# Weight loads between token tiles, gate weights behind the first projections, small loads moved to the last sequence

## The chip, the cores and the metric

The kernel runs on one core of a Trainium2 chip. The metric is device time in microseconds (us): the median of several executions. Engines are named as in the profile: PE (TensorE matmul), PEld (its weight load), DVE (VectorE), ACT (ScalarE), POOL (GpSimd), SP (SyncE, which here only issues transfers), and the 16 DMA engines.

## The reference, cut to what matters

```
x = x + window_attention(layernorm(x))            # 8 sequences of 512 tokens, width 256, 16 heads
x = x + cross_attention(layernorm(x), ctx, mask)
x = x + ffn(layernorm(x))

def ffn(x):                                       # attention runs over the 8 sequences at each position
    y = layer_norm(x + mha(x, Wqkv, bqkv, Wo, bo), g1, be1)
    logits = y @ Wg.T                             # 8 experts
    idx = argmax(logits)
    moe = relu(y @ W1[idx] + b1[idx]) @ W2[idx] + b2[idx]
    return layer_norm(y + moe, g2, be2)
```

All arithmetic is in float32, or in float32 split into bfloat16 parts. The kernel gets the gate's logits without y: it multiplies the gate weights into the output projection beforehand (`w_o[:, :, D:GATED]`, the "gated" columns) and sums them up (`gate_sums`).

## The kernel before, in words

Three programs follow one another, each a block in which the five engines run their own instruction lists and meet only at semaphores.

**Attention** (`attention_program`) goes over the sequences n = 0 to 7. SP issues all transfers in the order of its `iteration(n)`: the copy of the prefix values, the context, x for the layernorm two sequences ahead, x for the residual (`x_res`), the rows of the cross attention's queries (`stack_context_queries`), the rows of queries and keys of the first half of the heads of the next sequence (`stack_front(n, 0)`), the mask, one fill of the table `sorted` with empty rows (`fill_rows`, 4290 KB a time), the shift rows of the next sequence (`stack_shift`, two small transfers that PE's `window_shifted(n + 1, 0, 0)` waits for), the second half of the heads, and the context's keys. In sequence 0 the 31 loads of the next stage's constants (`later_loads`) stand between the mask and the fill, L529 to L531. ACT issues two small transfers of its own in each sequence (L1111, shift rows of the second half of the heads, for `window_shifted(n, 2, 0)`). Sequence 0 has no cross attention; that of sequence 7 and the tail of the window attention run in `closing`.

**Mixing** (`mixing_program`) goes over 8 groups of 512 tokens, n = 0 to 7, in a software pipeline. In `iteration(n)` PE does the transposes (`features`), the output projection of the group before (`output(n)`), queries and keys, `heads`, values, the scores of group n + 1 and the ranks that sort tokens by expert. DVE does the softmax, adds the residual (`mix`), takes layernorm statistics and chooses the expert; POOL takes rstd and logits and sends finished rows by indirect DMA (`send_rows`, four instructions for a group, on table positions that DVE's `slots` computes). PE, ACT and DVE pass results through two PSUM banks in a fixed order of names, `work_order`: a fill may start when the fill two places before it is read (`work_claim`).

Before group 0 stands the opening: `gate_weights()` on PE (transposes of w_o, L2489; totals, L2494; gated product, L2499), for which ACT takes the transposed w_o out of PSUM (`take_gates`, L2422) after it has written the position mask (L2444), which POOL makes; then 14 matmuls whose result nobody reads (`keep_warm(14)`, L2508), `features(-1)`, four projections and values of group 0. SP loads x of group m by eight transfers (`load_x`, L2017), each after DVE has normalised the group before, and the weights of expert n (`load_expert`, 2 MB in three transfers) after x of group n + 3. All experts must have landed before DVE builds the step tables that end the stage.

The last two groups run without a successor: PE goes through `output(7)`, `heads(7)`, `ranks(7)`, `output(8)`, and then the ranks in two halves; DVE's `last_route` does the same two halves.

**Experts** (`expert_program`) runs 39 steps of 128 rows each, PE-bound.

Of the kernel before, what the change touches and what calls it, by code (L numbers as in the profile page):

```python
# [142 lines left out]
def attention_program(nc, t, mem, later_loads, x_in, group_loaded, x2_stored, waits_passed):  # L143
# [3 lines left out]
    with ctx:  # L147
# [256 lines left out]
        with nc.Block() as block:  # L404

            @block.sync
            def _(sp):
# [88 lines left out]
                def tiles_of(src):  # L496
                    return src.rearrange("(c p) d -> p c d", p=P)
# [5 lines left out]
                def fill_rows(dst, count):  # L503
                    sp.dma_start(dst, filler[:, :].unsqueeze(1).broadcast_to([P, count, ROW])).then_inc(rows_filled.sem, 16)

                def iteration(n, last=False, ahead=True):
                    first = isinstance(n, int) and n == 0
                    copy_prefix(n)
                    if not first:
                        sp.wait_ge(ctxT_ready.sem, ctxT_ready.count(n, 0))  # L510
                    for rep in range(2):
                        sp.dma_start(ctx_in[rep * CTX:(rep + 1) * CTX, :], t["ctx"][n]).then_inc(ctx_loaded.sem, 16)
                    if ahead:
                        sp.wait_ge(ln_done.sem, ln_done.next(n, TILES))
                        load_x(n + 2)
                    if not first:
                        sp.wait_ge(x1_ready.sem, x1_ready.count(n, 2))
                    sp.dma_start(x_res[:, :, :], tiles_of(t["x"][n])).then_inc(xres_loaded.sem, 16)
                    if not first:
                        for tile in range(KD):  # L520
                            stack_context_queries(n, tile)
                    if not last:
                        stack_front(n, 0)
                    if not first:
                        stack_shift2(n)
                    if not first:
                        sp.wait_ge(mask_ready.sem, mask_ready.count(n, 1))
                    sp.dma_start(mask_in[:, :, :], tiles_of(t["mask"][n])).then_inc(mask_loaded.sem, 16)
                    if first:  # L529
                        for dst, src in later_loads:  # L530
                            sp.dma_start(dst, src).then_inc(later_loaded.sem, 16)  # L531
                        sp.wait_ge(consts_set.sem, 12)
                    fill_rows(t["sorted"][0:E * REGION, :].rearrange("(e p k) w -> e p k w", e=E, p=P)[n], REGION // P)
                    if last:
                        fill_rows(t["sorted"][E * REGION:, :].rearrange("(p k) w -> p k w", p=P), SPARE_TILES)
                    if not last:
                        stack_shift(n)
                        stack_front(n, 1)
                    if not first and not last:
                        store_x2(n)  # L540
                    split_context_keys(n)
# [1197 lines left out]

N_CONST = 6 + 5 + 4  # L1740
REGION = B * S + P
SPARE_TILES = 10
# [16 lines left out]
ROUTE_FILLS = ["out0", "out1", "out2", "out3", "ranks"]  # L1759
HALVES_FILLS = ["out0", "out1", "out2", "out3", "ranks0", "ranks1"]  # L1760
GATED = D + E
PROJECT_FILLS = ["xT0", "xT1", "q0", "q1", "k0", "k1", "v0", "v1", "v2", "v3"]
MIX_FILLS = ["xT0", "xT1", "out0", "out1", "out2", "out3", "q0", "q1", "k0", "k1", "v0", "v1", "v2", "v3", "ranks"]
OPENING_FILLS = [f for f in MIX_FILLS if f not in ROUTE_FILLS]
CLOSING_FILLS = [f for f in MIX_FILLS if f not in PROJECT_FILLS]
QUADS, QUAD = 4, 32
# [67 lines left out]
def mixing_program(nc, t, mem, consts, keep, ahead, x_in, group_loaded, x2_stored, waits_passed):  # L1834

    ctx = ExitStack()
    with ctx:
# [126 lines left out]
        def released(n, name):  # L1964

            kind, k = name.rstrip("0123"), int(name[-1]) if name[-1] in "0123" else 0
            sig, count = {
                "xT": (xT_ready, KD + k + 1), "q": (q_ready, KD + k + 1), "k": (k_ready, KD + k + 1),
                "v": (v_ready, TILES + k + 1), "out": (mixed_ready, k + 1), "ranks": (next_row_ready, k + 1),
            }[kind]  # L1970
            return sig.sem, sig.count(n, count)
# [6 lines left out]
        def work_filled(n, name):  # L1978

            return sum(len(work_order(m)) for m in range(-1, n)) + work_order(n).index(name) + 1  # L1980

# [4 lines left out]
        def work_claim(pe, n, name):  # L1986

            order = work_order(n)
# [21 lines left out]
        with nc.Block() as block:  # L2010

            @block.sync
            def _(sp):
# [13 lines left out]

                def iteration(n, more):
                    if more:
                        sp.wait_ge(ln_done.sem, ln_done.count(n, 3 * TILES))  # L2030
                        load_x(n + 3)
                    load_expert(n)

                sp.dma_start(keep["b1"][:, :], t["e_b1"]).then_inc(weights_loaded.sem, 16)
                sp.dma_start(tile_rows[:, :], t["c_tile_rows"]).then_inc(weights_loaded.sem, 16)
                sp.wait_ge(x2_stored.sem, x2_stored.count(B, 16))
                for m in range(2):
                    sp.wait_ge(ln_done.sem, ln_done.count(m, TILES))
                    load_x(m + 1)
                for n in range(NGROUPS):  # L2040
                    iteration(n, n < NGROUPS - 3)

# [112 lines left out]
            def _(dve):  # L2155
# [134 lines left out]
                def iteration(n, more=True):  # L2290
                    route = n > 0
                    shift_scores(n)
                    if n > 1:
                        slots(n - 1, whole, 0, "ranks")
# [3 lines left out]
                    if route:  # L2298
                        mix(n, 1)
                        mix(n, 2)  # L2300
                    normalise(n)
                    if route:
                        mix(n, 3)
                    turn(n)
                    keep_gate(n)
# [11 lines left out]
                def last_route(n):  # L2317
                    first_half, second_half = post_norm_parts(n)
                    for k, own in enumerate((first_half, second_half)):
                        for c in range(own.start, own.stop):  # L2320
                            mix(n, c)
                        post_norm_statistics(n, own)
                        post_norm_scale(n, own)
# [49 lines left out]
                for n in range(NGROUPS):  # L2373
                    iteration(n, more=n < NGROUPS - 2)
                slots(NGROUPS - 1, whole, 0, "ranks")
                last_route(NGROUPS)
# [3 lines left out]
            def _(act):  # L2380
# [37 lines left out]

                def take_gates():
# [4 lines left out]
                    act.wait_ge(gates_summed.sem, 2)  # L2424
                    nc.scalar.activation(w_o[:, :, D:GATED], ps_heads[:, 1, 0:KD * E].rearrange("p (k e) -> p k e", k=KD),
                                         ACT.Copy).then_inc(gates_ready.sem, 1)
                    nc.scalar.activation(gate_sums[:, :, :], ps_heads[:, 2, 0:3 * E].rearrange("p (i e) -> p i e", i=3),
                                         ACT.Copy).then_inc(gates_ready.sem, 1)

                def iteration(n, project=True):  # L2430
# [7 lines left out]
                    if project:  # L2438
                        values(n)

                act.wait_ge(mask_made.sem, 3)
                for r in range(QUADS):
                    own = slice(QUAD * r, QUAD * (r + 1))
                    nc.scalar.activation(mask_pos[own, :], own_position[own, :, :].rearrange("p i s -> p (i s)")[:, own],  # L2444
                                         ACT.Copy).then_inc(mask_made.sem, 1)
                take_gates()
                act.wait_ge(consts_set.sem, CONSTS_SET)
                features(-1)
                queries(-1)
                keys(-1)  # L2450
                values(-1)
                for n in range(NGROUPS):
# [6 lines left out]
            def _(pe):  # L2459
# [24 lines left out]

                def gate_weights():
# [5 lines left out]
                    mm.then_inc(gates_summed.sem, 1)  # L2491
                    pe.wait_ge(gates_made.sem, 4 * KD + 1)
                    for k in range(KD):
                        nc.tensor.matmul(ps_heads[:, 2, 0:3 * E], ones, gates[:, k, :, :].rearrange("p i e -> p (i e)"),  # L2494
                                         start=(k == 0), stop=(k == KD - 1), skip_group_check=True)
                    pe.wait_ge(gates_ready.sem, 1)
# [52 lines left out]

                def output(n):  # L2550
                    for c in range(TILES):
                        ps = work_claim(pe, n, f"out{c}")
# [23 lines left out]
                def iteration(n, project=True, route=True):  # L2576
# [12 lines left out]
                    if route:  # L2589
# [392 lines left out]
```

## Time and profile before

| what | value |
|---|---|
| median of 3 runs (lowest, highest) | 1214.45 us (1211.98, 1217.58) |
| profiled execution: own time, its span | 1213.34 us, 1211.3 us |
| busy: PE, DVE, ACT, POOL | 1112.3 (92%), 734.5, 478.9, 510.3 us |
| first instruction of mixing, of experts | 691.88 us, 912.45 us |
| fill of `sorted`, 4290 KB: median from issue to landing | 17.3 us |
| one row transfer `q_rows<-q_parts`, 128 KB | 2.4 us |
| one tile transfer `x_in<-x_rows`, 64 KB | 2.4 us |

Times inside the span count from its first instruction. In a row of the timeline the first number is the start, the second the duration, then engine, line, operation, what is written and read, and the number of instructions (x3); brackets give the idle time of that engine just before, and what ended it. A letter q behind an engine (SPq, ACTq) is its queue that issues transfers: the duration there is that of issuing.

### The profile page before, as it was taken

What the parts mean: (1) busy time and instruction counts of PE and PEld (TensorE: products, weight loads), DVE (VectorE), ACT (ScalarE), POOL (GpSimd) and SP (SyncE); (2) the same over time, 40 slices, a digit from 0 to 9 for tenths busy, and PEclk for the clock granted to TensorE, in tenths of its full rate; (3) what the DMA queues carried; (4) which work ended last, traced back from release to release, by engine and by line L of the source; (5) the groups of instructions that cost most, each with busy time, mean ns of one, the idle gap of its engine ahead of it and who ended that gap; (6) DMA issues with size and microseconds to landing.
All of it is one profiled execution on the core that took longest, in us unless ns stands there. A gap on an engine that the chain in (4) does not pass through costs nothing. (4 is left out here: it accounts for less than half of the span.)

```text
span 1211.3 us, 29502 instructions
## 1 busy us (share of the span) xinstructions
PE 1112.3 (92%) x10067; PEld 753.3 (62%) x10068; DVE 734.5 (61%) x2088; ACT 478.9 (40%) x866; POOL 510.3 (42%) x758
## 2 busy tenths in 40 slices
PE   8998899999999999999988889998879999999995
PEld 3545455464464554645554446656548999999994
DVE  4554676657756667576536436666574556566563
ACT  5444545454544545444452233233203333333330
POOL 3324425235244252442522022445363665556654
PEclk9999999999999999999999989889989999999998
DMA  7256563735546546336363113537213111111110
GB/s 220 71 155 166 147 188 106 201 102 144 154 116 173 155 112 189 102 106 189 105 182 88 56 36 98 183 107 273 78 51 93 50 49 50 49 51 56 50 44 7
DMA packets 143477, 137.95 MB, mean 114 GB/s; under 512 B 30376, under 2 KB 136750, under 8 KB 143280
## 3 DMA queue, kind: packets, MB, share of 16 engines
q1 hardware_dynamic: 137808, 124.20, 36.0%
q0 software_dynamic: 5280, 12.66, 3.2%
q8 instruction: 43, 0.70, 0.2%
q14 instruction: 26, 0.21, 0.1%
q10 hardware_dynamic: 320, 0.16, 0.1%
HBM read 49.38 MB, written 50.83 MB: 83 GB/s over the span
## 5 line engine op out<-in xcount | busy, mean ns | idle before, releaser
L970 ACT ACTIVATE probs<-ps_ab 128x512 f32<-128x512 f32 (+2 forms) x352 | 174.5, 537 | 95.3 <-PE ps_ab L1292 39.4
L591 POOL TENSOR_SCALAR_AFFINE_SELECT probs<-probs 128x512 f32<-128x512 f32 x128 | 81.7, 638 | 271.1 <-ACT probs L970 267.4
L2854 PE MATMUL ps_ab<-e_yT,e_w_now 128*128 128x128 f32 x1248 | 146.6, 276 | 0.0
L2854 PEld LDWEIGHTS ps_ab<-e_yT,e_w_now 128*128 128x128 f32 x1248 | 143.3, 193 | 0.5 <-ACT e_yT L2825 0.4
L2865 PE MATMUL ps_c<-keep_w,e_hT 128*128 x624 | 141.0, 379 | 0.0
L2865 PEld LDWEIGHTS ps_c<-keep_w,e_hT 128*128 128x128 f32 x624 | 115.7, 190 | 14.1
L712 DVE CUSTOM_DVE_ANT_0 ps_ab<-ps_ab,mask_qk 128x256 f32<-128x256 f32 x224 | 89.0, 451 | 18.8 <-PE ps_ab L1261 18.7
L1822 ACT ACTIVATE e_w_now<-keep_w 128x1024 f32 x78 | 78.2, 1049 | 40.1 <-issue 40.1
L706 DVE TENSOR_REDUCE top<-ps_ab 128x2 f32<-128x512 f32 (+1 forms) x112 | 74.2, 684 | 28.8 <-PE ps_ab L1261 28.0
L2789 DVE TENSOR_SCALAR e_hT<-ps_ab,keep_b 128x128 f32<-128x128 f32 x312 | 84.4, 343 | 8.5 <-PE ps_ab L2854 6.0
L1261 PE MATMUL ps_ab<-k_rows,q_rows 96*128 96x256 bf16 (+1 forms) x512 | 84.5, 260 | 4.6 <-DVE top L712 2.7
L2825 ACT ACTIVATE e_yT<-ps_d 128x256 f32<-128x256 f32 x39 | 15.0, 384 | 168.3 <-PE ps_d L2844 168.3
L1292 PE MATMUL ps_ab<-q_rows,k_rows 98*128 98x256 bf16 (+1 forms) x512 | 75.5, 260 | 0.2
L578 POOL TENSOR_TENSOR parts<-rest,parts 128x512 bf16<-128x512 f32 x32 | 38.0, 1189 | 82.7 <-ACT parts L960 82.7
L1261 PEld LDWEIGHTS ps_ab<-k_rows,q_rows 96*128 96x128 bf16 x512 | 39.9, 98 | 45.5 <-DVE top L712 12.3
L2766 POOL DMA_INDIRECT out<-e_result,e_token x39 | 41.8, 1072 | 60.5 <-DVE e_token L2785 43.9
L1335 PE MATMUL ps_c<-probs,v_ones 128*32 128x256 f32 (+1 forms) x1024 | 64.4, 359 | 0.0
L1219 PE MATMUL ps_d<-xT,w_qkv 128*128 128x512 f32 x128 | 62.6, 607 | 0.2
L2473 PE MATMUL ps_d<-e_w_now,m_w_qkv 128*128 128x512 f32 x128 | 56.4, 594 | 1.5 <-ACT e_w_now L2398 1.5
L594 POOL TENSOR_SCALAR_AFFINE_SELECT probs<-probs 128x256 f32<-128x256 f32 x128 | 56.7, 443 | 0.0
L2801 DVE TENSOR_TENSOR e_summed<-ps_c,e_yb 128x256 f32<-128x256 f32 x39 | 16.6, 425 | 62.9 <-PE ps_c L2865 62.9
L766 DVE RECIPROCAL rden<-rden 128x512 f32<-128x512 f32 x15 | 50.1, 3342 | 7.0 <-ACT rden L1000 7.0
(250 smaller groups left out, 2137.6 us busy)
## 6 DMA issues: line engine op xcount, KB each, us to landing
sorted_rows<-filler SPq DMA_DIRECT2D x8, 4290.0 KB, 17.3
q_rows<-parts SPq DMA_DIRECT2D x96, 128.0 KB, 2.4
k_rows<-parts SPq DMA_DIRECT2D x96, 128.0 KB, 2.4
q_rows<-q_parts SPq DMA_DIRECT2D x96, 128.0 KB, 2.4
keep_w<-in_e_w SPq DMA_DIRECT2D x16, 512.0 KB
keep_w<-in_e_w SPq DMA_DIRECT2D x8, 1024.0 KB
e_row<-sorted_rows SPq DMA_DIRECT2D x39, 130.0 KB, 2.1
x_in<-in_x SPq DMA_DIRECT2D x8, 512.0 KB, 3.9
```

The lines of the kernel that those rows point to most:

```text
L591: nc.gpsimd.affine_select(own, own, [[0, TILES], [1, P]], ALU.is_ge, keep_zero, base=0, channel_multiplier=-1).then_inc(probs_cut.sem, 1)
L706: nc.vector.tensor_reduce(top[:, c, first:first + heads], ps.rearrange("p (h k) -> p h k", h=heads), AX.X, ALU.max).then_inc(max_free.sem, 1)
L712: best = nc.vector.tensor_tensor_reduce(scores, scores, mask_qk[:, 1, :], 1.0, LEAST, ALU.add, ALU.max, top[:, c, first + i:first + i + 1])
L970: nc.scalar.activation(probs[:, user % 2, lo:lo + width], ps_exp[:, f % 2, 0:width], ACT.Exp).then_inc(exp_done.sem, 1)
L1219: mm = nc.tensor.matmul(ps, w_qkv[:, k, col:col + P], xT[:, k, :], start=(k == 0), stop=(k == KD - 1), skip_group_check=True)
L1261: mm = nc.tensor.matmul(ps[:, i * width:(i + 1) * width], q_rows[0:SPLIT_ROWS, k, q0:q0 + P], k_rows[0:SPLIT_ROWS, k, q0 + P - width:q0 + ...
L1292: mm = nc.tensor.matmul(ps[:, 256 * i:256 * i + q1 - q0], k_rows[:, h, kt * P:(kt + 1) * P], q_rows[:, h, q0:q1], start=(kt == 2), stop=Tr ...
L1335: mm = nc.tensor.matmul(ps_out[32 * j:32 * j + 32, g % 2, q0:q1], lhsT, rhs, start=(kt == order[0]), stop=True, skip_group_check=True)
L1822: nc.scalar.activation(self.w1_now[:, s, k, :], keep["w1"][:, k, bass.ds(e * DF, DF)], ACT.Copy).then_inc(self.w1_ready.sem, 1)
L2789: nc.vector.tensor_scalar(hT[:, s, f, :], ps_h[s][:, f // 4, (f % 4) * P:(f % 4 + 1) * P], b1[:, bass.ds(e * KF + f, 1)], 0.0, ALU.add, AL ...
L2854: mm = nc.tensor.matmul(ps_h[s][:, f // 4, (f % 4) * P:(f % 4 + 1) * P], w1_now[:, s, k, f * P:(f + 1) * P], yT[:, s, k * P:(k + 1) * P], ...
L2865: mm = nc.tensor.matmul(ps_out[:, s, 0:D], hT[:, s, f, :], w2[:, bass.ds(e * KF * D + f * D, D)], start=(f == 0), stop=(f == KF - 1))
```

## The change

Four parts: (1) the constants' loads leave sequence 0 and go in two lots, 13 and 18, around the queries' rows of sequence 7; (2) the gate weights are made in two steps, the product behind the first four projections, and ACT takes w_o before the mask; (3) SP loads the weights of expert n + 1 when `features(n)` are taken, and x of group n + 3 behind them; (4) in the last group DVE turns the probabilities before it mixes the third tile, and PE does half of `output(8)` before `ranks(7)`, with the fills and DVE's `slots(7)` moved to match.

```diff
@@ attention, SP, iteration(n)
                     sp.dma_start(x_res[:, :, :], tiles_of(t["x"][n])).then_inc(xres_loaded.sem, 16)
+                    if last:
+                        load_later(later_loads[:EARLIER])          # EARLIER = 13
                     if not first:
                         for tile in range(KD):
                             stack_context_queries(n, tile)
+                    if last:
+                        load_later(later_loads[EARLIER:])
...
                     if first:
-                        for dst, src in later_loads:
-                            sp.dma_start(dst, src).then_inc(later_loaded.sem, 16)
                         sp.wait_ge(consts_set.sem, 12)
@@ mixing, order of the PSUM fills
-HALVES_FILLS = ["out0", "out1", "out2", "out3", "ranks0", "ranks1"]
+HALVES_FILLS = ["out0", "out1", "ranks_held", "out2", "out3", "ranks0", "ranks1"]
-CLOSING_FILLS = [f for f in MIX_FILLS if f not in PROJECT_FILLS]
+CLOSING_FILLS = ["out0", "out1", "out2", "out3"]
@@ mixing, SP
-                for m in range(2):
-                    sp.wait_ge(ln_done.sem, ln_done.count(m, TILES))
-                    load_x(m + 1)
-                for n in range(NGROUPS):
-                    iteration(n, n < NGROUPS - 3)     # load_x(n + 3) after ln_apply(n + 2), then load_expert(n)
+                sp.wait_ge(ln_done.sem, ln_done.count(0, TILES))
+                load_x(1)
+                for n in range(-1, NGROUPS - 1):
+                    sp.wait_ge(xT_ready.sem, xT_ready.next(n, KD))
+                    load_expert(n + 1)
+                    if n < NGROUPS - 3:
+                        sp.wait_ge(ln_done.sem, ln_done.count(n, 3 * TILES))
+                        load_x(n + 3)
@@ mixing, DVE, iteration(n), closing = n == NGROUPS - 1
                     if route:
                         mix(n, 1)
+                        if not closing:
+                            mix(n, 2)
+                    normalise(n)
+                    if closing:
+                        turn(n)
                         mix(n, 2)
-                    normalise(n)
                     if route:
                         mix(n, 3)
-                    turn(n)
+                    if not closing:
+                        turn(n)
@@ mixing, DVE, last_route
                             mix(n, c)
+                        if k == 0:
+                            slots(n - 1, whole, 0, "ranks")
@@ mixing, ACT, opening
+                take_w_o_back()            # w_o transposed, and the totals
+                act.wait_ge(consts_set.sem, CONSTS_SET)
+                features(-1)
                 act.wait_ge(mask_made.sem, 3)
                 for r in range(QUADS):
                     ...                    # position mask
-                take_gates()
-                act.wait_ge(consts_set.sem, CONSTS_SET)
-                features(-1)
                 queries(-1)
                 keys(-1)
+                take_gated_w_o()
                 values(-1)
@@ mixing, PE, opening
-                gate_weights()
+                turn_w_o()
+                gate_totals()
                 keep_warm(14)
                 features(-1)
                 for j in range(4):
                     query_or_key(-1, j)
-                pe.wait_ge(gates_made.sem, 4 * KD + 1)
+                gated_w_o()
                 projected_values(-1)
@@ mixing, PE, end
-                output(NGROUPS)
+                output(NGROUPS, (0, 1))
+                ranks(NGROUPS - 1)         # before: at the end of iteration(NGROUPS - 1)
+                output(NGROUPS, (2, 3))
```

## Rows read from the trace of the kernel before

**Rows 1.** Timeline of SP's queue, sequence 0, behind the mask.
```profile
67.01 0.55 SPq L531 DMA_DIRECT2D m_identf<-in_c_identity  x1
...
84.77 0.65 SPq L504 DMA_DIRECT2D sorted_rows<-filler  x1
88.78 7.31 SPq L473 DMA_DIRECT2D q_rows<-shiftT  x2
```

**Rows 2.** Timeline of SP's queue, the same two steps in sequence 1.
```profile
149.71 0.66 SPq L504 DMA_DIRECT2D sorted_rows<-filler  x1
166.50 1.42 SPq L473 DMA_DIRECT2D q_rows<-shiftT  x2
```

**Rows 3.** Timeline of PE: start and a later step of sequence 1, then of sequence 2.
```profile
102.37 0.23 PE L1288 MATMUL ps_ab<-mask_first,ident 128*128 128x128 bf16 x1 [4.05 <-DMA q_rows<-shiftT]
...
129.38 0.28 PE L1299 MATMUL ps_ab<-mask_prefix,ident 128*128 128x256 bf16 x1 [0.21 <-ACT probs L970]
...
182.82 0.22 PE L1288 MATMUL ps_ab<-mask_first,ident 128*128 128x128 bf16 x1
...
209.04 0.28 PE L1299 MATMUL ps_ab<-mask_prefix,ident 128*128 128x256 bf16 x1 [0.20 <-ACT probs L970]
```

**Rows 4.** Busy times by window: length, PE, PEld, DVE, ACT, POOL, granted clock, DMA share, GB/s.
```profile
102.40:107.50 5.10, 5.02 (x30) 3.89 (x31) 0.68 (x2) 3.35 (x7) 2.00 (x4) 0.67 0.92 211
```

**Rows 5.** Timeline of ACT's queue and of PE, sequence 0, second half of the heads.
```profile
66.58 1.93 ACTq L1111 DMA_DIRECT2D q_rows<-shiftT  x2
...
72.28 0.22 PE L1288 MATMUL ps_ab<-mask_first,ident 128*128 128x128 bf16 x1
```

**Rows 6.** Timeline of SP's queue in sequence 7, and of PE at its queries' second tile.
```profile
590.71 0.59 SPq L518 DMA_DIRECT2D x_res<-in_x  x1
598.14 7.74 SPq L461 DMA_DIRECT2D q_rows<-q_parts  x12
616.16 1.22 SPq L467 DMA_DIRECT2D q_rows<-shiftT  x2
...
610.74 0.38 PE L1419 MATMUL ps_ab<-mask_add,ident 128*128 128x512 bf16 x1 [0.28 <-DVE top L738]
```

**Rows 7.** Timeline of PE, DVE and ACT in the opening of mixing.
```profile
693.34 0.62 PE L2494 MATMUL ps_ab<-m_gates,e_w_now 128*128 128x24 f32 x4 [0.50 <-DVE m_gates L2218]
...
696.57 1.62 DVE L109 TENSOR_SCALAR m_xn<-x_in,m_moments,m_rstd 128x256 f32<-128x256 f32 x4 [1.44 <-POOL m_rstd L103]
...
698.77 0.60 ACT L2422 ACTIVATE e_w_now<-ps_ab 128x512 f32<-128x512 f32 x1
...
699.42 1.88 PE L2499 MATMUL ps_ab<-m_gates,e_w_now 128*128 128x8 f32 x8 [5.45 <-ACT e_w_now L2422]
...
701.15 4.79 PE L2508 MATMUL ps_c<-m_before,m_ident 128*128 128x512 bf16 x14
...
707.61 4.56 PE L2473 MATMUL ps_d<-e_w_now,m_w_qkv 128*128 128x512 f32 x10 [0.80 <-ACT e_w_now L2398]
```

**Rows 8.** Busy times by window, columns as in rows 4: the opening, then two groups.
```profile
699.40:705.60 6.20, 6.18 (x22) 3.41 (x23) 0.00 (x0) 0.27 (x2) 1.43 (x2) 0.59 0.30 89
...
826.10:850.00 23.90, 20.68 (x330) 14.25 (x327) 15.87 (x51) 7.18 (x13) 10.76 (x16) 0.93 0.98 344
850.00:872.70 22.70, 20.63 (x326) 14.12 (x324) 12.58 (x39) 7.18 (x13) 9.79 (x14) 0.92 0.20 69
```

**Rows 9.** Timeline of DVE's statistics of groups 1 and 2, and PE's group 1.
```profile
705.60 1.40 DVE L92 BATCH_NORM_STATS2 m_stats<-x_in 128x6 f32<-128x256 f32 x4 [7.41 <-DMA x_in<-x_rows]
...
724.60 1.40 DVE L92 BATCH_NORM_STATS2 m_stats<-x_in 128x6 f32<-128x256 f32 x4
...
735.47 1.09 PE L2466 MATMUL ps_d<-m_identf,m_xn 128*128 128x128 f32 x8
```

**Rows 10.** Timeline of DVE in the last two groups.
```profile
876.43 0.43 DVE L2208 TENSOR_TENSOR m_mixed<-ps_d,m_xnb 128x264 f32<-128x264 f32 x1 [0.32 <-PE ps_d L2556]
...
893.79 0.88 DVE L2250 SCALAR_TENSOR_TENSOR m_rows<-m_mixed,m_rstd,m_be 128x256 f32<-128x256 f32 x2 [2.07 <-POOL m_rstd L2083]
```

More of the change, by code:

```diff
@@ L504, in fill_rows, with load_later @@
                     sp.dma_start(dst, filler[:, :].unsqueeze(1).broadcast_to([P, count, ROW])).then_inc(rows_filled.sem, 16)
+                def load_later(loads):
+                    for dst, src in loads:
+                        sp.dma_start(dst, src).then_inc(later_loaded.sem, 16)
                 def iteration(n, last=False, ahead=True):
@@ L1740 @@
 N_CONST = 6 + 5 + 4
+EARLIER = 13
 REGION = B * S + P
@@ L1969, in released @@
                 "v": (v_ready, TILES + k + 1), "out": (mixed_ready, k + 1), "ranks": (next_row_ready, k + 1),
+                "ranks_held": (next_row_ready, 0),
             }[kind]
@@ L1978, in work_filled @@
         def work_filled(n, name):
+            if name == "ranks" and n == NGROUPS - 1:
+                n, name = NGROUPS, "ranks_held"
             return sum(len(work_order(m)) for m in range(-1, n)) + work_order(n).index(name) + 1
@@ L1986, in work_claim @@
         def work_claim(pe, n, name):
+            if name == "ranks" and n == NGROUPS - 1:
+                n, name = NGROUPS, "ranks_held"
             order = work_order(n)
@@ L2026, in load_expert @@
                                  t["e_w2"][e].rearrange("(j p) d -> p j d", p=P)).then_inc(weights_loaded.sem, 16)
[L2028 to L2032, printed above, removed]
                 sp.dma_start(keep["b1"][:, :], t["e_b1"]).then_inc(weights_loaded.sem, 16)
@@ L2292, in iteration @@
                     shift_scores(n)
+                    closing = n == NGROUPS - 1
                     if n > 1:
@@ L2374, in _ @@
                     iteration(n, more=n < NGROUPS - 2)
-                slots(NGROUPS - 1, whole, 0, "ranks")
                 last_route(NGROUPS)
@@ L2417, in values, with take_w_o_back @@
                         nc.scalar.activation(v[:, c, :], ps[:, 0:GATED], ACT.Copy).then_inc(v_ready.sem, 1)
-                def take_gates():
+                def take_w_o_back():
                     act.wait_ge(gates_summed.sem, 1)
@@ L2424, in take_gates, with take_gated_w_o @@
                     act.wait_ge(gates_summed.sem, 2)
+                    nc.scalar.activation(gate_sums[:, :, :], ps_heads[:, 2, 0:3 * E].rearrange("p (i e) -> p i e", i=3),
+                                         ACT.Copy).then_inc(gates_ready.sem, 1)
+                def take_gated_w_o():
+                    act.wait_ge(gates_summed.sem, 3)
                     nc.scalar.activation(w_o[:, :, D:GATED], ps_heads[:, 1, 0:KD * E].rearrange("p (k e) -> p k e", k=KD),
-                                         ACT.Copy).then_inc(gates_ready.sem, 1)
-                    nc.scalar.activation(gate_sums[:, :, :], ps_heads[:, 2, 0:3 * E].rearrange("p (i e) -> p i e", i=3),
                                          ACT.Copy).then_inc(gates_ready.sem, 1)
@@ L2483, in projected_values, with turn_w_o @@
                         mm.then_inc(work_full.sem, 1)
-                def gate_weights():
+                def turn_w_o():
                     for j in range(KD):
@@ L2491, in gate_weights, with gate_totals, gated_w_o @@
                     mm.then_inc(gates_summed.sem, 1)
+                def gate_totals():
                     pe.wait_ge(gates_made.sem, 4 * KD + 1)
                     for k in range(KD):
-                        nc.tensor.matmul(ps_heads[:, 2, 0:3 * E], ones, gates[:, k, :, :].rearrange("p i e -> p (i e)"),
-                                         start=(k == 0), stop=(k == KD - 1), skip_group_check=True)
+                        mm = nc.tensor.matmul(ps_heads[:, 2, 0:3 * E], ones, gates[:, k, :, :].rearrange("p i e -> p (i e)"),
+                                              start=(k == 0), stop=(k == KD - 1), skip_group_check=True)
+                    mm.then_inc(gates_summed.sem, 1)
+                def gated_w_o():
                     pe.wait_ge(gates_ready.sem, 1)
@@ L2548, in heads, with output @@
                     mm.then_inc(heads_full.sem, 1)
-                def output(n):
-                    for c in range(TILES):
+                def output(n, tiles=range(TILES)):
+                    for c in tiles:
                         ps = work_claim(pe, n, f"out{c}")
@@ L2588, in iteration @@
                         scores(n + 1)
-                    if route:
+                    if route and project:
                         ranks(n)
```

## The prediction

> **What bounds the kernel now.** I read the page first: PE is busy for 92% of the span, so the question at each edit is whether PE stands still there, and for what. The chain that ended last lies wholly in the expert stage, which the change does not touch; any gain must come before it and shift it. The waits of PE and the timelines by stage then show two standstills that the change aims at. In sequence 1 PE starts with 4.05 us of waiting for the shift rows [rows 3]; in the opening of mixing it waits 5.45 us for ACT's copy of w_o [rows 7]. Both are followed by a low clock: 0.67 in the 5.1 us behind the first [rows 4], 0.59 in the 6.2 us behind the second [rows 8]; 2.4 GHz is granted elsewhere, 1.2 GHz in parts of these.
>
> **Part 1, the constants' loads.** In sequence 0 the 31 loads take SP from 67.01 to 84.77, 17.76 us, 0.57 each. Only then is the fill issued; 4.0 us later SP starts the shift rows, which take 7.31 us to issue behind it [rows 1]. In sequence 1 the fill goes out 16.8 us before the shift rows, and their issue takes 1.42 us [rows 2]. Without the loads the fill of sequence 0 is issued at about 67.0 and, at its 17.3 us, has landed at 84.3, before 88.78. Issued in 1.4 us and landing 2.4 us later (the figure of the other row transfers), the shift rows are there at 92.6; PE wants them at 98.3 (102.37 less 4.05). So the wait goes as a whole: 4.05 us. The clock: from its first instruction to L1299 sequence 1 takes 27.01 us, sequence 2 takes 26.22 [rows 3]; the 0.79 us between them is the low clock as far as PE's other partners let it count. Bounds for the two together: 4.05 (no clock gain), and 4.05 + 5.1 x 0.33 = 5.7 (all of it). I take 4.8, from the comparison of like sequences.
>
> In sequence 7 the first 13 loads (7.4 us) start at 591.30 and end at 598.7 to 599.2, so the queries' rows start 0.6 to 1.1 us late. Their last is now issued by 605.88 and used from 610.74 [rows 6]: 4.9 us less 2.4 of landing leaves 2.5, enough. The 18 others (10.3 us) end near 617.2, so the shift rows of 616.16 start about 1 us late; what is late next are the mask, the two last fills and the context's keys, all issued behind them for PE work of the closing. I cost this at nothing; if the cover were gone it costs its 1.1 us.
>
> **Part 2, the gate weights.** ACT now takes w_o first, so PE goes on from the totals, which end at 693.96, straight into the 14 matmuls. These took 4.79 us at a clock of 0.59; I keep that, and they end at 698.75. The normalised x is ready at 696.57 + 1.62 = 698.19, so it no longer matters. From the end of the 14 to the first projection it was 707.61 - 705.94 = 1.67 us; the first projection moves to 700.42, by 7.2 us [rows 7]. The product stands now behind the projections and costs PE time there: eight instructions, 1.88 us at the low clock, 1.24 if they run like the totals (four in 0.62) [rows 7]. I take 1.24, since the clock is full from 705.6 on. ACT's copies of the mask (four) fall between x and the first query, while PE runs 1.7 us of projection. Net 5.9 us. Bounds: at full clock the 14 end before 698.19 and x decides, 0.56 more, 6.5; if the low clock reaches into the projections for some 3.5 us, that costs 1.7 and the product its 1.88: 3.5 to 3.8, lower bound 3.5.
>
> **Part 3, the weights.** In the steady groups nothing moves: after x of a group SP finds `features` taken and issues one expert as before, only two experts further on. What changes is both ends. At the start expert 0 goes out behind x of group 1 (from about 704), ahead of x of group 2, which is requested when group 1 is normalised, near 710.4. In the group where four experts were issued together the DMA engines moved 344 GB/s [rows 8]; at that rate 2 MB take 6.1 us and are through by 713, so x of group 2 meets only the end of it. x of group 1 came 7.4 us after its request (698.19 to 705.60 [rows 9]), so x of group 2 lands at 717.8, with the weights at 720 at worst. DVE wants it at 724.60 - 5.9 = 718.7; its statistics and scaling need 4.8 us, and PE wants the result at 735.47 - 5.9 = 729.6 [rows 9]. Slack 4.8 us: nothing is lost. At the end the four experts are no longer issued at once. The group beside that burst lasts 23.9 us, the next 22.7, with the same 20.6 to 20.7 us of PE work [rows 8]. Bounds 0 and 1.2 us; I take 0.6, for its granted clock was no lower.
>
> **Part 4, the last groups.** DVE no longer waits 0.32 us for the third output before it normalises [rows 10]; turning one `mix` (0.43) earlier brings PE's `heads(7)` and half of `output(8)` forward by some us. But in the last group DVE stands 2.07 us for POOL's rstd before 893.79 [rows 10]. POOL is busy until then with the six sends that its list puts ahead of that rstd, and this part takes none of them away; only their start, behind DVE's statistics, moves by the 0.32. Also `slots(7)`, now behind two `mix` (0.9 us), is done 2 us or more before that rstd. I take 0.3 us; bounds 0 and 0.8.
>
> **Sum.** 4.8 + 5.9 + 0.6 + 0.3 = 11.6 us off the execution that was profiled, 1213.34 us (span 1211.3 and 2.0 around it): 1201.7. The median of the runs shown is 1.1 higher, so the forecast is 1202.8 us. With all lower bounds the sum is 7.5 (1207), with all upper ones 14.2 (1200.3). A measurement here tells a change from none at about 0.5%, 6.1 us.
>
> **Rivals.**
> (a) *The clock keeps half of it.* The low clock moves onto the projections, and the stretch behind the first wait gains nothing: 4.05 + 3.5 + 0 to 0.6, so 1206 to 1207. For it: both standstills were followed by low clock although PE was busy in it. Against: the new opening has no PE gap of more than half a microsecond behind 693.96. Chance 0.12.
> (b) *x comes late.* The fill moves 4290 KB in 17.3 us, 248 GB/s. If weights from memory got half of that beside the tiles, 2 MB would take 17 us, x of group 2 (512 KB) would land near 727, its result at 732, 2.4 us after PE wants it, and group 3's may repeat it: 2.4 to 6 us, 1205 to 1209. Against it: x of group 1 is issued ahead of all weights. Chance 0.07.
> (c) *The other side: the early fill stops ACT's shift rows.* ACT issues them from 66.58 to 68.51 and PE uses them at 72.28 [rows 5]; the new fill is issued at 67.0. Behind a fill on SP's own queue the like pair took 7.31 us to issue and held PE up [rows 1, 3]. If ACT's pair had to wait it out as well, it would land after 84.3 and PE stand 12 us, and lose 1.7 of clock: 1216.5. It decides from a stall of 11.6 us up; one of 2 to 3 us costs just that. Against it: it is another queue, and half of the pair is issued before the fill. Chance 0.05.
> The Trainium skill, "DMA: Bandwidth & Descriptors", section "Queues, rings and completion order", says that a DMA engine takes turns between its queues, one whole packet of descriptors each (9 to 17 typical, 64 at most). By that rule the pair waits for a packet or two of the fill, not for all of it; no row here has the two side by side, and the sum would stay.
> (d) *The groups give it back.* In both groups of rows 8 PE idles for 2 to 3 us and the clock falls (23.90 less 20.68, 22.70 less 20.63) [rows 8]. If the new phase lengthens that by 1 to 2 us in each of five groups, 5 to 9 us return: 1207 to 1211. Nothing in the change moves the sends against the scores within a group. Chance 0.07.
>
> **How the numbers follow.** Forecast, 1199 to 1207: 0.66; (a) 0.12, (b) 0.07, (c) 0.05, (d) 0.07, and 0.03 for a slowdown over 0.5% that I do not see. The range 1197.5 to 1208.5 takes in (a), most of (b) and half of (d), and leaves out about 0.15. Faster by over 0.5% (below 1208.4): 0.66 + 0.12 + 0.05, and 0.01 of (d): 0.84. Within: 0.12. Slower: 0.04.
>
> **What would show it.** Right: no DMA wait of PE at the start of sequence 1, SP's two shift transfers issued in under 2 us, PE's first L1288 there at 98.3 and not 102.37; PE without a gap over 1 us between the totals and the first projection, that one at about 695.6 (4.8 + 7.2 earlier); x of group 2 awaited by DVE for no more than 2 us; experts starting near 901. Wrong: a PE wait for shift rows near 72, a gap before `features(1)` in mixing, more PE idle time in the later groups, or a DMA wait of PE in sequence 7.

## The result, and the profile after

| | before | changed |
|---|---|---|
| median of 10 runs (lowest, highest) | 1216.67 us (1211.98, 1218.13) | 1207.41 us (1203.19, 1208.41 and one of 2705) |
| profiled execution: own time, its span | 1213.34, 1211.3 us | 1207.58, 1205.6 us |
| first `features(1)` matmul of mixing | 735.47 us | 726.43 us |
| ranks of group 6 (`ranks(6)`) | 872.49 us | 866.57 us |

The ratio is 0.9926, 95% interval 0.9912 to 0.994: 9.0 us off (7.3 to 10.7), where 11.6 were forecast. The ratio leaves out the one execution of the changed kernel that took 2705 us; the median of its nine others is 1207.25. The two profiled executions stand only 5.7 us apart, since that of before was low among its runs. Two lines of the page of the changed kernel:

```profile
span 1205.6 us, 29501 instructions
...
PE 1113.7 (92%) x10067; PEld 754.1 (63%) x10068; DVE 734.2 (61%) x2088; ACT 478.6 (40%) x866; POOL 509.7 (42%) x758
```

PE is as busy as before; what moved is where it stands still. The timelines of SP, ACT and PE in sequences 0 and 1 of the changed kernel, against [rows 1, 3, 5]:

```profile
67.21 0.63 SPq L504 DMA_DIRECT2D sorted_rows<-filler  x1
91.64 1.49 SPq L473 DMA_DIRECT2D q_rows<-shiftT  x2
...
66.54 1.93 ACTq L1117 DMA_DIRECT2D q_rows<-shiftT  x2
...
74.17 0.29 PE L1294 MATMUL ps_ab<-mask_first,ident 128*128 128x128 bf16 x1 [1.78 <-DMA q_rows<-shiftT]
...
101.02 0.22 PE L1294 MATMUL ps_ab<-mask_first,ident 128*128 128x128 bf16 x1
...
127.20 0.28 PE L1305 MATMUL ps_ab<-mask_prefix,ident 128*128 128x256 bf16 x1 [0.21 <-ACT probs L976]
...
144.12 0.39 PE L1262 MATMUL ps_ab<-mask_qk,ident 128*128 128x512 bf16 x1 [1.65 <-DMA k_rows<-parts]
...
612.97 0.23 PE L1294 MATMUL ps_ab<-mask_first,ident 128*128 128x128 bf16 x1 [0.70 <-DMA q_rows<-shiftT]
```

The fill goes out at 67.2, SP's shift rows take 1.49 us to issue, and the wait of 4.05 us at the start of sequence 1 is gone. But a new one stands at 74.17: ACT's pair is behind the fill. The packets of its second transfer run from 70.4 to 73.1 us, where in the kernel before they were through by 69.4. So PE is at L1305 only 2.2 us sooner (127.20 for 129.38). The row at 144.12 is a wait that every kernel has (before: 1.45 us at 146.10); the last one, in sequence 7, is new.

The opening of mixing, timeline of PE and one row of DVE, against [rows 7, 9]:

```profile
691.15 0.62 PE L2518 MATMUL ps_ab<-m_gates,e_w_now 128*128 128x24 f32 x4 [0.50 <-DVE m_gates L2227]
691.62 3.18 PE L2536 MATMUL ps_c<-m_before,m_ident 128*128 128x512 bf16 x14
694.85 1.97 PE L2487 MATMUL ps_d<-m_identf,m_xn 128*128 128x128 f32 x8
697.61 7.13 PE L2494 MATMUL ps_d<-e_w_now,m_w_qkv 128*128 128x512 f32 x16 [0.80 <-ACT e_w_now L2414]
704.58 0.95 PE L2527 MATMUL ps_ab<-m_gates,e_w_now 128*128 128x8 f32 x8
...
726.43 1.09 PE L2487 MATMUL ps_d<-m_identf,m_xn 128*128 128x128 f32 x8
...
702.77 1.41 DVE L92 BATCH_NORM_STATS2 m_stats<-x_in 128x6 f32<-128x256 f32 x4 [6.77 <-DMA x_in<-x_rows]
```

From the totals to `features(1)` it is 35.28 us, before 42.13: 6.85 off. The 14 unread matmuls run in 3.18 us, not 4.79: with no standstill ahead of them the clock stays at 2.4 GHz (1.00 from 691.6 to 694.9).

With 9.04 us in hand at 726.43 the changed kernel has 5.92 left at `ranks(6)`. The windows view of one of the groups between, and its scores in the timelines of PE and POOL:

```profile
795.40:820.20 24.80, 22.28 (x327) 15.31 (x324) 15.77 (x51) 7.18 (x13) 10.91 (x16) 0.84 0.39 126
```
```profile
815.35 0.69 PE L2555 MATMUL ps_c<-e_w_now 64*32 64x32 f32 x43
816.50 0.28 PE L2555 MATMUL ps_c<-e_w_now 64*32 64x32 f32 x6 [0.45 <-issue]
817.24 0.25 PE L2555 MATMUL ps_c<-e_w_now 64*32 64x32 f32 x4 [0.47 <-issue]
818.15 0.33 PE L2555 MATMUL ps_c<-e_w_now 64*32 64x32 f32 x3 [0.66 <-issue]
818.87 1.12 PE L2555 MATMUL ps_c<-e_w_now 64*32 64x32 f32 x72 [0.40 <-issue]
...
813.03 1.12 POOL L2125 DMA_INDIRECT sorted_rows<-m_rows,m_slot  x1 [0.64 <-issue]
814.45 0.96 POOL L2125 DMA_INDIRECT sorted_rows<-m_rows,m_slot  x1 [0.30 <-issue]
815.72 0.96 POOL L2125 DMA_INDIRECT sorted_rows<-m_rows,m_slot  x1 [0.30 <-issue]
816.99 0.96 POOL L2125 DMA_INDIRECT sorted_rows<-m_rows,m_slot  x1 [0.30 <-issue]
```

"issue" means that the profile names nothing that PE waited for. The 128 small matmuls of `scores` stop four times, while POOL sends rows; then the clock falls and the next group's first matmuls run at half speed. Before had this too: up to `ranks(6)` such gaps in the scores add up to 9.5 us in 17 pieces there, and to 10.3 us in 19 after, 1.2 of it in `scores(2)`. The five groups from `ranks(1)` to `ranks(6)` take 118.2 us before, 119.8 after, and the group ahead of them 19.0 and 20.6. So in the five groups the gaps are no longer than before (9.1 us for 9.5); PE idles for 13.3 us in them for 13.4, and is busy 1.7 us longer (106.5 for 104.8), at a granted clock of 0.90 for 0.91.

In the last group DVE waits 4.92 us for POOL's rstd, where it had waited 2.07 [rows 10]; the statistics came earlier, POOL's answer did not:

```profile
887.60 0.88 DVE L2259 SCALAR_TENSOR_TENSOR m_rows<-m_mixed,m_rstd,m_be 128x256 f32<-128x256 f32 x2 [4.92 <-POOL m_rstd L2092]
```

### The profile page after: what moved, and what is told of

Same layout as the page of the kernel before. It is cut to its first block and busy times, and to the rows that moved or that the text cites. A ratio compares the mean times of both kernels' runs of the same rounds, so it can differ in the third digit from the quotient of the medians.

```text
span 1205.6 us, 29501 instructions
## 1 busy us (share of the span) xinstructions
PE 1113.7 (92%) x10067; PEld 754.1 (63%) x10068; DVE 734.2 (61%) x2088; ACT 478.6 (40%) x866; POOL 509.7 (42%) x758
## 5 line engine op out<-in xcount | busy, mean ns | idle before, releaser
L2896 PEld LDWEIGHTS ps_c<-keep_w,e_hT 128*128 128x128 f32 x624 | 115.7, 190 | 14.1
L1298 PEld LDWEIGHTS ps_ab<-q_rows,k_rows 98*128 98x128 bf16 x512 | 41.9, 99 | 21.3 <-ACT probs L976 9.4
```

Source lines behind the costliest of these rows:

```text
L1298: mm = nc.tensor.matmul(ps[:, 256 * i:256 * i + q1 - q0], k_rows[:, h, kt * P:(kt + 1) * P], q_rows[:, h, q0:q1], start=(kt == 2), stop=Tr ...
L2896: mm = nc.tensor.matmul(ps_out[:, s, 0:D], hT[:, s, f, :], w2[:, bass.ds(e * KF * D + f * D, D)], start=(f == 0), stop=(f == KF - 1))
```

## The experiments

Times off are ratios times the median of before on the same chip: 1203.8 us for the first four, 1203.4 for the next four, 1215.8 for the last four; in brackets the 95% interval.

### Each part alone

The kernel before with the lines of one part of the diff.

> The kernel before with part 1 alone (the constants' loads leave sequence 0 and go in two lots in sequence 7). The prediction's step says 4.8 us less than before, and no wait of PE for shift rows near 72 us. The theory read from the trace of the changed kernel says: SP's wait of 4.05 us is gone, but ACT's second shift transfer now lands behind the fill's first packets, PE waits 1.5 to 2 us at about 74 us and runs at half clock for some 3 us behind it, and only 2.0 to 2.5 us are gained in all. A rival: the low clock after that wait is not part 1's doing but luck of the execution; then the PE wait is there and 3.0 to 3.5 us are gained.

Off: 3.5 us [1.0 to 6.0]. Timeline of PE in this kernel:

```profile
74.33 0.23 PE L1294 MATMUL ps_ab<-mask_first,ident 128*128 128x128 bf16 x1 [1.85 <-DMA q_rows<-shiftT]
...
607.88 0.39 PE L1425 MATMUL ps_ab<-mask_add,ident 128*128 128x512 bf16 x1 [0.95 <-DMA q_rows<-q_parts]
```

The new wait is part 1's. Here no low clock followed it, and L1305 comes at 126.39, 2.99 us sooner: the rival that priced it without the clock. In the interval lie that and 4.8 too; for this one execution the trace decides. The second row is a wait that I had costed at nothing: sequence 7's queries' rows, behind the 13 loads.

> The kernel before with part 2 alone (totals first, gated product behind the first projections, ACT takes w_o ahead of the mask). The prediction's step says 5.9 us less than before (3.5 to 6.5). The theory read from the trace of the changed kernel says 6.5 to 7: the 14 unread matmuls run at full clock in 3.2 us and not in 4.8. The rival by which the clock keeps half says 3.5. First projection of mixing 7 to 10 us after the totals, where before it was 14.

Off: 7.1 us [4.9 to 9.4]. The 14 matmuls take 3.18 us again, and from the totals to `features(1)` it is 35.18 us. The forecast was 1.0 low; rival (a) is out for this execution.

> The kernel before with part 3 alone (weights of an expert ahead of x of the next group but one, and no burst of four at the end). The prediction's step says 0.6 us less (0 to 1.2). The theory read from the trace of the changed kernel: the group beside the former burst is no shorter, so 0 gained there; and if the 1.5 us that group 1 lost in the changed kernel (PE idle for no named cause in the scores of group 2) come from the weights that now start there, this kernel is 1 to 1.5 us slower than before. If that loss is not part 3's, no change, within 0.3 us.

Off: 1.1 us [-1.0 to 3.3], too wide to size it. `scores(2)` runs without a gap, so the 1.2 us lost there in the changed kernel is not part 3's: that reading of mine falls. The group beside the former burst takes 20.06 us from ranks to ranks; in parts 1 and 2 alone, with the burst, 21.01 each. All these groups have the sends beside them as well, so the difference of 1 us need not be the burst's alone.

> The kernel before with part 4 alone (turn ahead of the mix of the third tile in the last group; half of the output projection of the last group ahead of its predecessor's ranks). The prediction's step says 0.3 us less (0 to 0.8). Rival from the trace of the changed kernel: PE now stands 3.2 us before the first half of the last ranks and runs its next stretch at half clock, which takes back what was gained: no change, or up to 0.5 us slower.

Off: 0.5 us [-2.0 to 2.9]. From `ranks(7)` to `ranks0` it takes 14.05 us; the five other kernels with the old order (before, parts 1, 2 and 3 alone, and the tenth run) have 14.31 to 14.41. The rival of a longer wait is half right: PE waits 3.07 us before `ranks0`, where it had waited 1.80; but from there to the second half it takes 2.19 us in both. The profiled execution, 1214.9 us, is the longest of the twelve, and its five groups from `ranks(1)` to `ranks(6)` take 116.7 us, where the first three runs have 106.3 to 109.1.

### The fill held, the sends moved

> The changed kernel itself, beside the next three on the same chip. If its parts add up (part 1 alone 3.1 us, part 2 alone 6.5 to 7.1, parts 3 and 4 together 0 to 1.6, by ratios and traces), it is 10 to 11.5 us under the kernel before; if the parts disturb each other in the groups of mixing, about 9, as in the first comparison.

Off: 9.4 us [6.1 to 12.6], with single executions from 1189.8 to 1199.1. PE's wait at 74 is 2.14 us and 6.8 us of 1.2 GHz follow it.

```diff
                     if first:
                         sp.wait_ge(consts_set.sem, 12)
+                        sp.wait_ge(shift_stacked[1].sem, shift_stacked[1].count(n, 32))
                     fill_rows(...)
```

> The changed kernel with one wait more: in sequence 0 SP issues the fill only when ACT's two shift transfers have landed, near 69.5 us. If the fill's packets are what delays the second of them, the wait of PE at 74 us (1.8 us) is gone, the next transposed rows come 1.8 to 2.9 us sooner, and the time is 1.9 us under that of the changed kernel, up to 2.9 with the clock. If the delay is ACT's queue's own, the wait stays and the time is that of the changed kernel. The fill still lands by 87 us, and SP's shift rows are issued behind it without a new wait at the start of sequence 1.

Off: 15.3 us [13.0 to 17.6], executions from 1187.5 to 1190.3. Windows view of the same 4.6 us, first the changed kernel, then this one (the last three columns are clock, DMA share, GB/s), and this one's timelines:

```profile
68.40:73.00 4.60, 3.62 (x24) 1.55 (x21) 3.65 (x7) 1.23 (x2) 1.15 (x1) 1.00 1.06 321
```
```profile
68.40:73.00 4.60, 4.22 (x31) 2.25 (x29) 3.66 (x7) 1.48 (x3) 1.15 (x1) 1.00 0.43 144
```
```profile
69.82 0.64 SPq L504 DMA_DIRECT2D sorted_rows<-filler  x1
88.72 1.92 SPq L473 DMA_DIRECT2D q_rows<-shiftT  x2
...
98.09 0.22 PE L1295 MATMUL ps_ab<-mask_first,ident 128*128 128x128 bf16 x1
...
693.05 8.83 PE L2495 MATMUL ps_d<-e_w_now,m_w_qkv 128*128 128x512 f32 x16 [0.80 <-ACT e_w_now L2415]
```

Where the fill filled the DMA engines (share 1.06, 321 GB/s) ACT's pair, 8 KB each, now finds them half idle. PE does not wait at 74 nor at 98.09, the time that the prediction gives for it (98.3). In the four kernels with the hold, L1305/6 comes at 124.28 to 124.46; in the five with the early fill (the first, fifth, seventh, eighth run and the changed kernel) at 126.39 to 128.59, mean 127.6: the early fill costs 3.2 us. At the totals, the first matmuls of mixing that use the gate weights, the same nine profiles stand at 686.6 to 688.2 and at 690.0 to 693.1: 3.9 us on average. The median here is 7.1 us under that of the changed kernel on the same chip, more than that; between the two profiles 3.6 us arise behind `ranks0`, where the two kernels are alike, and why is open. The last row shows rival (a): the 16 projections take 8.83 us and not 7.13, half clock over 3.4 us of them. It is so in this and the eleventh run; the seven other profiles of kernels with part 2 have 7.13.

```diff
                     iteration(n, ahead=n < NGROUPS - 1, more=n < NGROUPS - 2)
+                    if n < NGROUPS - 1:
+                        wait_apart(pool, pool_passed, scores_full.sem, scores_full.count(n + 1, 1))
                     send_rows(n - 1)
```

> The changed kernel, but in groups 2 to 6 POOL sends the rows of the group before only when PE has finished the scores of the next group. If PE's idle time in the scores (1 to 2.3 us a group, with no releaser named) comes from these sends, it goes, the half clock behind it too, and five groups of up to 24 us become 21 us each: 5 to 12 us under the changed kernel. If the idle time is PE's own supply of instructions, it stays, and the time is that of the changed kernel or up to 2 us more, since the sends may now hold up POOL's bias and rstd.

Off: 13.7 us [10.5 to 17.0]; its median is 7.8 us under that of the changed kernel. Windows view of a group, and its scores and sends in the timelines:

```profile
786.10:806.70 20.60, 18.88 (x328) 12.49 (x324) 16.88 (x51) 7.18 (x13) 10.95 (x16) 1.00 0.48 155
```
```profile
794.45 5.39 PE L2496 MATMUL ps_d<-e_w_now,m_w_qkv 128*128 128x512 f32 x12 [0.63 <-DVE m_mixed L2219]
...
805.16 1.42 PE L2557 MATMUL ps_c<-e_w_now 64*32 64x32 f32 x128
...
791.14 0.96 POOL L2125 DMA_INDIRECT sorted_rows<-m_rows,m_slot  x1 [0.30 <-issue]
792.12 1.28 POOL L2085 TENSOR_TENSOR m_xnb<-m_xn,m_b_o 128x512 f32<-128x512 f32 x1
```

The 128 matmuls run in one piece, the clock is 1.00 over the group, and it takes 20.6 us for 24.8 in the first profile of the changed kernel. On this chip the difference is smaller: the five groups take 101.6 us, in the fifth run 107.1. What is left of the sends is the end of the last one at 792.1, straight behind which POOL does the bias that DVE needs; PE waits 0.6 to 0.9 us for that.

```diff
-                        nc.gpsimd.indirect_dma_start(out=t["sorted"], ..., in_=rows[...]).then_inc(rows_sent[...].sem, 16)
+                        nc.gpsimd.memset(unsent[...], 0.0).then_inc(rows_sent[...].sem, 16)
```

> The changed kernel without the transfers of finished rows: POOL writes a few zeros in place of each, so the sorted table keeps its empty rows and the expert stage works on those. Only the groups of mixing are to be compared. If the sends cause PE's idle time in the scores, none of it is left; if PE's supply of instructions does, it stays in place, with the same half clock behind it.

This kernel leaves out the sending of finished rows, so its time (1177.4 us) is not compared. No gap in the scores of groups 3 to 7, clock 1.00 in all of them, and a group takes 19.5 us:

```profile
784.80:804.30 19.50, 18.60 (x326) 12.52 (x323) 15.55 (x51) 7.18 (x13) 7.08 (x16) 1.00 0.41 137
```

But one gap of 0.95 us stays, in `scores(2)`, where nothing is sent in any kernel. Timelines of PE there, in the changed kernel and in that with the fill held:

```profile
744.24 1.06 PE L2555 MATMUL ps_c<-e_w_now 64*32 64x32 f32 x101
746.52 0.34 PE L2555 MATMUL ps_c<-e_w_now 64*32 64x32 f32 x27 [1.22 <-issue]
```
```profile
740.92 1.48 PE L2556 MATMUL ps_c<-e_w_now 64*32 64x32 f32 x128
```

In all 14 traces this gap goes with an instruction load on the DMA queue (16 KB records of the queue `q8 instruction` in narrow windows): where the load that follows the one at 10.6 to 11.3 us behind the group's first matmul starts 14.1 to 14.2 us behind it, the group takes 19.0 us (before, and the third, sixth, seventh, ninth, tenth and twelfth run); where it starts at 17.1 to 17.5 there is the gap of 0.95 to 1.22 and the group takes 20.0 to 20.6. Kernels with and without part 3 stand on both sides. What sets the moment of the load stays open, and so does whether the late load causes the gap: nothing was run that moves it.

### Both additions, and what they lay bare

The changed kernel with the two diffs above.

> The changed kernel with both additions: the fill of sequence 0 held until ACT's shift transfers have landed, and POOL's sends of groups 2 to 6 behind the scores. If the two are independent, the gains add: 7 us for the first (1.9 to 2.9 of it by the traces, the rest from the groups) and 7 to 8 for the second, but what the first gained in the groups can't be gained twice, so 10 to 12 us under the changed kernel, 18 to 21 under the kernel before.

Off: 28.9 us [25.8 to 32.2] on a chip where before takes 1215.8. Its median, 1185.7, and those of the last two runs, 1186.1 and 1185.3, are the lowest of all kernels that compute the whole. I had expected 18 to 21. The groups disturbed by the sends seem to cost more on this chip: the next run gains 17.3 us by moving them, the seventh had gained 7.8.

The second diff alone, in the kernel before.

> The kernel before, with nothing of the change, but with POOL's sends of groups 2 to 6 behind the scores. If the disturbance by the sends is a trait of the kernel and not of the change, 7 to 9 us under the kernel before, with no idle time of PE in the scores of the groups and no half clock behind them. If the change brought it, no gain.

Off: 17.3 us [14.5 to 20.1], so the disturbance is not the change's. On this chip the two lines of the seventh run give more than the change gave in any comparison (9.0 and 9.4 us); where both were tried on one chip, in the seventh run, they gave less, 7.8. In its profile the five groups from `ranks(1)` to `ranks(6)` take 102.7 us, in that of before, from the first comparison, 118.2. Its windows view, two groups, the second beside the burst of four experts; then the second group in the ninth run, without the burst:

```profile
794.76:815.36 20.60, 18.90 (x329) 12.51 (x325) 16.89 (x51) 7.18 (x13) 10.92 (x16) 1.00 0.48 155
815.36:836.75 21.39, 18.98 (x328) 12.49 (x325) 16.70 (x51) 7.18 (x13) 10.76 (x16) 1.00 0.84 283
```
```profile
802.22:822.51 20.29, 18.77 (x328) 12.40 (x325) 16.70 (x51) 7.18 (x13) 10.75 (x16) 1.00 0.51 156
```

The ninth run with SP's loop of the kernel before.

> The kernel with both additions, with part 3 taken out again (weights behind x of two groups on, four experts at once at the end). In groups that the sends no longer disturb, part 3's own worth shows: by the prediction's step 0.6 us more than with both additions (0 to 1.2); by the trace of part 3 alone 0, within 0.5 us. A group beside the burst longer than its neighbours by 1.2 us would speak for the prediction's reading.

Off: 31.0 us [28.8 to 33.2]; median 0.4 over that with both additions, not to be told from it. The group beside the burst takes 21.47 us from ranks to ranks, its neighbours 20.59 and 20.29. With part 3 (seventh, ninth, twelfth run) it takes 20.29 to 20.31. Part 3 is worth 1.2 us in that group, the prediction's upper bound; in the medians it does not show.

The ninth run with the last groups in the order of the kernel before.

> The kernel with both additions, with part 4 taken out again (old order in the last group). By the prediction's step 0.3 us more than with both additions (0 to 0.8); if the longer gap of PE before the last ranks takes it back, the same or up to 0.5 us less.

Off: 31.0 us [28.7 to 33.2]; median 0.5 under that with both additions: no difference. From `ranks(7)` to `ranks0` 14.32 us, with part 4 (seven profiles, the changed kernel among them) 14.05 to 14.08. That 0.3 us is there; but over the two stretches from `ranks(6)` to `ranks0` the twelfth and the ninth run take 27.55 and 27.54 us, so in this pair nothing of it arrives. The eleventh run, with part 4, has 27.13 there, and with the sends in their old place it is 26.86 to 27.13 with part 4 and 27.14 to 27.41 without (four profiles each). So some 0.3 us arrives there; with the sends moved it is not settled.

## Why the prediction was right, and where it was off

The kernel got faster by 9.0 us, within the range, and the main steps hold. Of the prediction's signs of being right, the wait at the start of sequence 1, the two shift transfers, the opening without a gap over 1 us and x of group 2 came out; but two of its four signs of being wrong came too: a wait for shift rows near 72 (at 74.17) and a DMA wait in sequence 7. PE's first L1288 came at 101.02 and not 98.3, the first projection at 697.61 and not 695.6, the experts at 906.7 and not 901. By its terms:

- **Part 1, 4.8 us forecast, 3.0 at best, 2.2 in the changed kernel.** The wait of 4.05 us went as forecast, and with the fill held the whole step is worth its 4.8: L1305/6 comes at 124.4 (mean of four), 5.0 us ahead of the profile of before and 5.7 ahead of the mean of the five kernels with the old order (129.1 to 131.5). At the totals the old order stands at 693.2 on average, the early fill at 691.2, the held one at 687.3: 2.0 us for part 1 as it is, 6.0 with the fill held. What failed is the sentence that rests on the fill's start at 67.0 without pricing what it meets: it is rival (c), given 0.05, in its mild form. ACT's second transfer lands behind the fill's first packets and PE waits 1.8 to 2.1 us, in four of five executions with half clock behind it, 3.4 to 6.8 us long; together 3.2 us at L1305/6. The sixth run shows the cause: with the fill held the wait is gone. It is not the 12 us of the rival. The Trainium skill, "DMA: Bandwidth & Descriptors", section "Queues, rings and completion order", with its turns of one packet for each queue, would have a short wait there; the measured one agrees in that it is a tenth of the fill's 17.5 us. Sequence 7, costed at nothing, cost 0 to 0.95 us: 0.70 us of wait for shift rows in the changed kernel, 0.95 for the queries' rows in part 1 alone, none in the ninth run. A wait that the prediction does not name stands in all 14 profiles at 141 to 148: 0.93 to 1.93 us for `k_rows`. Behind it the clock was 0.74 in the changed kernel (143.5 to 150.0) and 1.00 in that of before (144.0 to 150.0), so a part of what was gained by then goes again in some executions.
- **Part 2, 5.9 forecast, 6.9 measured.** Right in mechanism. I kept the row of 4.79 us for the 14 matmuls and so the half clock that the standstill had caused, though the standstill was what the change took away; at 3.18 us x decides, the upper bound of 6.5 that the prediction names, and the product took 0.95 us, not 1.24, which makes the rest. Rival (a) is real, but rare and smaller: 1.7 us in two of nine profiles.
- **Part 3, 0.6 forecast, 1.2 in undisturbed groups**, nothing to be seen in the changed kernel, whose groups are disturbed by more. x of group 2 was in time: DVE's statistics started at 715.56 without a wait.
- **Part 4, 0.3 forecast, 0.3 measured** between the last ranks, too little for any median to show; the bound was POOL's rstd, as said: DVE now waits for it 4.92 us.
- **The groups (rival (d)).** The prediction gave 0 to the groups between and a chance of 0.07 that they give something back. In the profiled pair they returned 3.1 us: 1.55 in the group of `scores(2)`, 1.6 in the next five. The rival's place was right. The disturbance as such is not the change's, since the tenth run shows it in the kernel before, and the changed kernel itself takes 119.8 us for the five groups in one profile and 107.1 in another; whether the change adds a little to it can't be told from that.

The sum of what is shown: 2.2 + 6.9 + 0.3, less 3.1 for the groups, is 6.3. The two profiled executions are 6.2 us apart at `ranks0`, and 5.7 at the end, since the part behind it took 0.5 us longer. The medians stand 9.0 apart; which groups were disturbed in those executions no trace tells, so how near 9.0 comes to 11.6 is in part luck: part 1 fell short by 2.6 us, part 2 gave 1.0 more, and the groups vary by more than either.

## What to carry to other kernels

When a large transfer is moved forward, look at every small transfer of any queue that is in flight there and has a reader within a few us; hold the large one until they have landed, here for 2.6 us of 17. When a change takes away a standstill, price what runs behind it at the clock of an undisturbed row. And a row of "issue" gaps in an engine with many small instructions is worth one experiment that moves the transfers issued by another engine away from it: here it was worth 7.8 us on one chip and 17.3 on another.

## What the runs showed of the hardware

- PE's stream of 128 small matmuls with their weight loads stops while POOL issues four indirect transfers of 130 KB, though they share no data and no semaphore: for 1.2 to 2.3 us in sum in each of the five groups in the profiles of before and of the changed kernel, for 0 to 1.2 us in those of the first six runs. There some of the 128 also take longer without a gap that is listed (2.95 us for all of them in a group of the fifth run, 1.42 in the seventh). It never stopped when the sends were elsewhere (25 groups in the seventh, ninth, tenth, eleventh and twelfth run, but for one gap of 0.9 to 1.0 us beside the burst in the tenth and eleventh). How much differs by execution: groups of 19.8 to 23.1 us in one profile (the fifth run), 22.9 to 25.5 in another (the changed kernel). Whether it is POOL's work on the descriptors or their packets was not tried apart.
- The kernel before had medians of 1216.7, 1203.8, 1203.4 and 1215.8 us in the four comparisons. With the sends moved it took 1198.2 where it had 1215.8; in the second comparison the three profiled kernels that have its groups or part 3's (the first to the third run) have groups 0.7 to 3.8 us shorter than the profile of before, at fewer gaps. But the fourth run, on the same chip and with the same groups as before, has a profile of 1214.9 us with groups of 21.4 to 24.0 us, while its median is 1203.1. So this disturbance differs between executions, and its share seems to differ between chips; a profile of the kernel before on each chip would show the latter, and there is none.
- The clock fell to 1.2 GHz for 3.4 to 6.8 us behind a wait of PE of 1.8 to 2.1 us in four executions (the changed kernel, granted clock 0.51 from 73.9 to 77.4, and the fifth, seventh and eighth run) and not in another (the first run, a wait of 1.85 us, clock 1.00) at the same place.
